# ScalarE's order inside a unit: first eviction, relu for two units ahead, second eviction, in place of the relu and then both evictions

## What is computed

```python
def _L0_gnn_ref(x, adj, W1, b1, W2, b2, gamma, beta):
    hi = einsum('bsh,hk->bsk', x, W1[:H])
    hj = einsum('bsh,hk->bsk', x, W1[H:])
    h = relu(hi[:, :, None, :] + hj[:, None, :, :] + b1)
    y = einsum('bijk,kl->bijl', h, W2) + b2
    y = _layernorm(y, gamma, beta)
    return einsum('bij,bijh->bih', adj, y)

x = _layernorm(x + L0(x, adj))
x = _layernorm(x + L1(x, adj))     # one attention head, weights exp(si + sj) * adj
```

## Time and profile before

| what | value |
|---|---|
| median of 3 executions | 2302.32 us (2300.99 to 2302.67) |
| the profiled execution, device time | 2303.22 us |
| its span, first to last instruction | 2301.4 us |
| mean granted TensorE clock | 0.998 |
| TensorE matmuls busy | 2280.2 us, 99% |
| TensorE weight loads busy | 2075.6 us, 90% |
| ScalarE busy | 2160.9 us, 94% |
| VectorE busy | 2145.2 us, 93% |
| GpSimd busy | 2016.9 us, 88% |

### The profile page before, as it was taken

The page is one execution under the profiler, slowest core; times in us unless marked ns, Lnnn a source line. Parts: engine busy times, 40 slices in busy tenths (PEclk is TensorE's granted clock), DMA queues, the critical chain, the costliest instruction groups (busy, mean ns, idle before and its releaser), DMA issues.

```text
span 2301.4 us, 168989 instructions
## 1 busy us (share of the span) xinstructions
PE 2280.2 (99%) x71248; PEld 2075.6 (90%) x71248; DVE 2145.2 (93%) x18262; ACT 2160.9 (94%) x3650; POOL 2016.9 (88%) x1227
## 2 busy tenths in 40 slices
PE   8999999999999999999999999999999999999997
PEld 8888888888888999999999999999999999999995
DVE  7999999999999999999999999999999999999998
ACT  8999999999999999999999999999999999999996
POOL 9898898888988988888888898898888988888884
PEclk9999999999999999999999999999999999999999
DMA  1000000000000000000000000000000000000000
GB/s 21 12 13 16 11 16 16 10 16 12 15 16 10 16 16 11 16 12 15 16 11 16 13 13 16 11 16 16 10 16 13 14 16 10 16 17 10 16 10 10
DMA packets 103862, 32.15 MB, mean 14 GB/s; under 512 B 77888, under 2 KB 103104, under 8 KB 103104
## 3 DMA queue, kind: packets, MB, share of 16 engines
q1 hardware_dynamic: 102240, 21.12, 4.4%
q10 hardware_dynamic: 864, 0.23, 0.0%
HBM read 17.11 MB, written 4.19 MB: 9 GB/s over the span
## 4 chain that ended last, share of the span: by engine, by line
PE 97%; ACT 2%; DVE 1%; POOL 0%; issue 0%; DMA 0%; SPq 0%; DVEq 0%; ACTq 0%
PE y_ps L567 76%; PE agg_ps L618 19%; PE work_ps L567 2%; ACT h L294 1%; ACT y L289 1%; POOL h L278 0%; DVE squares L553 0%; DMA b1c<-in_L_gnn_b_dram 0%; DVE o_sb L465 0%; DVE x_out L545 0%; POOL wz L269 0%; SPq L172 0%; DVE work_ps L483 0%; DVE work_ps L530 0%; DVE work_ps L479 0%
## 5 line engine op out<-in xcount | busy, mean ns | idle before, releaser
L278 POOL TENSOR_TENSOR h<-abT 128x1024 f32<-128x1024 f32 x1024 | 1944.0, 1919 | 239.3 <-PE y_ps L567 231.9
L567 PEld LDWEIGHTS y_ps<-w_pair,h 128*32 128x32 f32 x65536 | 1920.4, 110 | 173.6 <-issue 126.5
L567 PE MATMUL y_ps<-w_pair,h 128*32 128x128 f32 x65536 | 1966.0, 273 | 1.3 <-issue 0.6
L553 DVE CUSTOM_DVE_ANT_0 squares<-y_ps,y 128x128 bf16<-128x128 f32 x8192 | 1839.0, 284 | 110.4 <-ACT y L289 103.4
L289 ACT ACTIVATE y<-y_ps 128x508 f32<-128x508 f32 x2048 | 1137.5, 596 | 104.6 <-PE y_ps L567 97.6
L294 ACT ACTIVATE h<-h 128x1024 f32<-128x1024 f32 x1024 | 1089.3, 1064 | 2.4 <-POOL h L278 2.4
L553 DVE DVE_READ_ACCUMULATOR2_ANT q<- 128x1 f32 x8192 | 678.5, 83 | 0.0
L618 PE MATMUL agg_ps<-y,wz 128*32 128x512 f32 x4096 | 593.4, 592 | 3.2 <-DVE work_ps L483 3.1
L618 PEld LDWEIGHTS agg_ps<-y,wz 128*32 128x32 f32 x4096 | 180.4, 110 | 9.1 <-issue 9.1
L567 PEld LDWEIGHTS work_ps<-x1s,adjS 128*32 128x32 f32 x512 | 28.4, 110 | 31.5 <-issue 18.9
L252 POOL TENSOR_TENSOR wz<-adjT,rstd 128x128 f32<-128x128 f32 x64 | 34.8, 543 | 25.0 <-ACT rstd L325 25.0
(11 more groups left out here) (87 smaller groups left out, 591.3 us busy)
## 6 DMA issues: line engine op xcount, KB each, us to landing
adj_in<-in_adj_dram SPq DMA_DIRECT2D x256, 16.0 KB, 1.9
x_res<-in_x_dram SPq DMA_DIRECT2D x64, 64.0 KB, 2.1
adj_res<-in_adj_dram SPq DMA_DIRECT2D x64, 64.0 KB, 2.7
out_dram<-x_out SPq DMA_DIRECT2D x64, 64.0 KB, 1.9
x_in<-in_x_dram SPq DMA_DIRECT2D x254, 16.0 KB, 1.9
w1a<-in_L_gnn_W_dram SPq DMA_DIRECT2D x1, 64.0 KB, 1.9
w1b<-in_L_gnn_W_dram ACTq DMA_DIRECT2D x1, 64.0 KB, 2.2
w<-in_L_gnn_W_dram ACTq DMA_DIRECT2D x1, 64.0 KB, 2.3
```

Source lines behind the costliest of these rows:

```text
L278: nc.gpsimd.tensor_tensor(h[:, u % HRING].rearrange("k (r g) s -> k r g s", g=GROUPS), abT[:, p, 1, :].unsqueeze(1).unsqueeze(1).broadcast ...
L553: last = nc.vector.tensor_tensor_reduce(out=squares[:, (first_bank + k) % YRING, n, :], in0=y_ps[(first_bank + k) % YRING][:, n, :], in1=y ...
L567: last = nc.tensor.matmul(dst[cols], lhsT[:, cols], rhs, start=start, stop=stop, tile_position=(0, g * GROUP))
```

## The change

ScalarE's relu for unit u+2 moves from ahead of the unit's other work to between the unit's two evictions. No instruction is added or removed, no wait changes, and the other engines' programs stay as they are. The new order in a unit is: the unit's other work if it has any, E(2u), R(u+2), E(2u+1).

```diff
             def slot(t, half, p, pairs, prep, gather, tail, early, first_bank):
                 for u in range(UNITS):
-                    if pairs:
-                        ahead = u + 2
-                        if ahead < UNITS:
-                            relu(t, ahead)
-                        elif prep:
-                            relu(t + 1, ahead - UNITS)
                     if gather and u == 1:
...
                             act.wait_ge(y_in_psum, t * QUARTS + k + 1)
                             copy(y[:, p, k * QUART:(k + 1) * QUART, 0:LAST],
                                  y_ps[(first_bank + k) % YRING][:, :, 0:LAST]).then_inc(y_stored, 1)
+                            ahead = u + 2
+                            if k == u * QPU and ahead < UNITS:
+                                relu(t, ahead)
+                            elif k == u * QPU and prep:
+                                relu(t + 1, ahead - UNITS)
```

## The result

| | before | after |
|---|---|---|
| median of 4 executions each | 2302.29 us | 2336.1 us (2335.28 to 2336.51) |
| ratio after to before | | 1.0147, 95% interval 1.0136 to 1.0159 |
| span of the profiled execution | 2301.4 us | 2334.7 us |
| one slot in the middle | 35.47 us | 36.00 us |

The change costs 33.8 us. The forecast was 2345.9 us with a range of 2334 to 2356. The sign and the place were right; a slot loses 0.53 us, not 0.70.

The account below looks back on a forecast made before the run. The prediction took TensorE to bound the middle. A loss of 62 x 0.70 = 43.4 us plus 0.2 in the last slot, 43.6 us, on the median of 2302.32 gave 2345.9 us, range 2334 to 2356.

Parts of the forecast that it names:

- What bounds the kernel: Middle, 48.9 to about 2269 us: TensorE alone, 35.47 us a slot, so reordering ScalarE can only cost.
- R2 falls behind E0's wait, and R4 comes too late: Slot's start: ScalarE waits at E0 with R2 still to do; R4 lets unit 4 start 0.68 us late.
- The first rival: Relu late by one eviction only, hidden by 0.72 us of slack; time 2302 to 2303 us; chance 0.07.
- The steps from E0 to R4: ScalarE, units 0 to 2: relus 0.95, evictions 0.485, ln_v and rstd 0.60, beta_part 0.29 us; 1108.72 to 1114.99.
- The step after the wait: TensorE's start after a wait: 1.78 us to the next sum, not 1.746, adding 0.03 us a slot.
- When TensorE wants R4: Unit 4 due at 1114.36 in the slot starting at 1107.38; 0.72 us of slack for R4 before the change.
- R3's lateness: Unit 3: R3 lets TensorE go on 0.2 us late, contained in R4's 0.68.
- Slots times loss: Slots t = 2 to 63: 62 x 0.70 = 43.4 us.
- The last slot: Tail, units 11 to 13: VectorE gains 0.4 us, then waits and ends 0.2 us later; +0.2 us.
- E22: ScalarE's eviction, first of unit 11 in the last slot, at 2268.78; the count for units 11 to 13 goes from it.
- The rival of a second wait: R6 also late if single evictions or restarts cost more: 0.9 to 1.3 us a slot, 2358 to 2383 us; chance 0.06.
- R5, R6 and the banks: Other deadlines in the slot, claimed not late: slack 0.7 us for R5, 0.5 for R6, 1.4 for the bank.

Follow-up runs that it names:

- the run with unit 0 old: Kernel after the change, with the old order (R2, E0, E1) put back in unit 0 of each slot; 2304.54 us, ratio 1.0003 to the kernel before.
- The run with unit 2 new and one spare eviction: Kernel before, with the new order in unit 2 alone and one eviction that nobody reads ahead of E2; 2325.33 us, ratio 1.0096.
- the run with unit 1 old: Kernel after the change, with the old order (R3, ln_v, rstd, E2, E3) put back in unit 1 of each slot; 2335.2 us, ratio 1.0139 to the kernel before.

## Why the prediction was right, and where it was off

**What bounds the kernel**: right. TensorE fills the middle, and the reordering could only cost.

**R2 falls behind E0's wait, and R4 comes too late**: right, shown by the chain after and by the run with unit 0 old, which takes away this alone and gives all of the loss back. The first rival, a relu late by one eviction and hidden, would have been true without the wait for E0, but not by its own numbers. Without that wait R4 still moves behind `beta_part` and E4, and not by one eviction: in the run with unit 0 old it ends 6.87 us after the first matmul, and 154.20 - 148.15 = 6.05 before. These 0.82 us are more than the 0.72 of slack that the prediction had, and less than the 0.88 that R4 has.

**The steps from E0 to R4**: right to some hundredths. From E0's start to R4's end I had 1114.99 - 1108.72 = 6.27 us. After the change, E0 and R4 in the timeline of ScalarE:

```profile
1122.44 0.59 ACT L289 ACTIVATE y<-y_ps 128x508 f32<-128x508 f32 x1 [0.47 <-PE y_ps L566]
...
1127.63 1.06 ACT L294 ACTIVATE h<-h 128x1024 f32<-128x1024 f32 x1
```

And the same slot in the timeline of TensorE:

```profile
1121.25 7.24 PE L566 MATMUL y_ps<-w_pair,h 128*32 128x128 f32 x256
1128.75 1.95 PE L566 MATMUL y_ps<-w_pair,h 128*32 128x128 f32 x64 [0.25 <-ACT h L294]
1130.52 1.04 PE L617 MATMUL agg_ps<-y,wz 128*32 128x512 f32 x8
```

1128.69 - 1122.44 = 6.25 us. The evictions that stand singly cost 0.47 to 0.49 us, as in pairs. The Trainium skill's formula ("ScalarE: Activation LUTs", What ACT_TABLE_LOAD costs), from which the prediction estimated 0.516 us for an eviction, is not borne out here either. The step after the wait cost 1130.52 - 1128.75 = 1.77 against 1.746, 0.02 where I had 0.03. (The prediction's 0.68 and 0.03 add up to 0.71 and not to 0.70, which is 0.6 us in 62 slots.)

**When TensorE wants R4**: this is the term that was mis-sized. I took 1107.38 from the earlier trace rows as the first matmul's start and 1108.72 as E0's, 1.34 us apart. In the kernel after they are 1121.25 and 1122.44, 1.19 apart. An earlier slot of the kernel before began at 148.15, and the timeline of ScalarE there and in the last pair slot has E0 at:

```profile
149.34 0.59 ACT L289 ACTIVATE y<-y_ps 128x508 f32<-128x508 f32 x1
...
2245.05 0.59 ACT L289 ACTIVATE y<-y_ps 128x508 f32<-128x508 f32 x1
```

149.34 - 148.15 is 1.19 again. In the slot that I chose, 319 matmuls stand in one piece, the 320th stands among the sums, and the 8 sums fall into groups of 3 and 5. That is not the order of the program, so the rows of matmuls don't stand where they belong there, and TensorE's starts lie 0.15 us early against ScalarE's. No record is missing: the whole trace has 65536 of these matmuls, as many as the program. The expectations call a slot without such a mixture one with complete records. The length of a slot is not touched by this, but a distance between two engines is. With 0.15 us more, unit 4 is 0.52 us late and a slot loses about 0.54, and the trace has 0.53. The run with unit 2 new and one spare eviction bears it out: 0.37 us late, in a slot whose rows are in order. R3's lateness was too large by the same 0.15 us: the prediction had 0.2. In the run with unit 1 old, where R3 is on time, the first four units take 7.17 us and not 7.24, so R3 costs 0.07 us. As the prediction says, this is a part of unit 4's lateness and not a cost on top.

**Slots times loss**: from E0 to E0, the 59 slots from 149.34 to 2245.05 took 35.52 us each before and the 60 slots from 114.45 to 2274.71 (E0 of the last pair slot) took 36.00 each after. The 0.05 us over 35.47 are the 3 us of small stops that the earlier trace rows left over; in the kernel after they are nearly gone. Whether its waits took them in or there were none in this execution stays open. The prediction counted the loss from 35.47 and so did not have these 3 us. So the middle costs 62 x 0.484 = 30.0 us.

**The last slot**: VectorE's part was right. The chain of the kernel after, from E22 on:

```profile
2298.91 0.59 ACT y L289
...
2312.14 0.37 DVE work_ps L482
...
2312.64 7.32 PE agg_ps L617 x40
```

From E22's start to the end of `bias_added` it is 13.60 us; before it was 2282.10 - 2268.78 = 13.32. So 0.3 later, where I had 0.2. But then TensorE's last 40 sums took 7.32 us. Before, the rows of `bias_added` and of these sums read:

```profile
2281.73 0.37 DVE work_ps L483
2282.24 4.50 PE agg_ps L618 x40
```

Busy time of two stretches of the kernel before (PE, PEld, DVE, ACT, POOL), then TensorE's granted clock and two columns on DMA; the first stretch is TensorE's idle time, the second those sums:

```profile
2279.20:2282.20 3.00, 0.00 (x0) 0.00 (x0) 2.72 (x11) 1.08 (x3) 1.20 (x3) 1.00 0.00 0
2282.20:2287.00 4.80, 4.76 (x52) 1.98 (x56) 1.79 (x8) 1.10 (x4) 0.00 (x0) 1.00 0.00 0
```

The same two in the kernel after:

```profile
2309.40:2312.60 3.20, 0.00 (x0) 0.00 (x0) 2.89 (x12) 1.08 (x3) 1.20 (x3) 0.84 0.04 11
2312.60:2320.30 7.70, 7.66 (x52) 2.33 (x56) 1.84 (x9) 1.10 (x4) 0.00 (x0) 0.62 0.00 0
```

The granted clock was 1.00 there before and 0.62 after, which is 2.8 us. The sum is 30.0 + 0.3 + 2.8 = 33.1 us, against 33.3 between the two spans.

**That the number fell inside the range was partly luck.** The prediction says nothing of the clock in the tail. The measured 2336.1 us lie 2 us above the lower end of the range, 2334. The profiled execution had 2336.51, and without the 2.8 us of the clock it would have had 2333.7 (an estimate), just outside. The run with unit 1 old has the same slot of 36.00 us, and its profiled execution, with 4.50 us for the last 40 sums, took 2333.95. The mis-sized term is worth 62 x 0.15 = 9 us and the small stops 3 us, both too much in the forecast; the tail gave 2.8 us back.

**The rival of a second wait**: it did not come in the changed kernel, but a candidate was nearer than my text knew. I had checked R5, R6 and the banks, and not the sum's wait for `bias_added`. The change moves E4 ahead of R4 and so makes this deadline easier, from 0.25 us of slack to 0.85. E4 ends 6.5 us after the first matmul, not 6.8, and `bias_added` ends at 1129.52 in the slot shown above, whose sum starts at 1130.52 (1130.52 - 0.15 - 1129.52 = 0.85):

```profile
1129.16 0.36 DVE L482 SCALAR_TENSOR_TENSOR work_ps<-bias_rows,agg_ps,work_ps 128x128 f32<-128x128 f32 x1
```

That it stayed harmless was luck in the prediction.

## What to carry to other kernels

An instruction that stands ahead of a wait may be free, and behind the wait it costs in full: ask of a moved instruction what its engine did at that moment, not how many places it moves. List every deadline that the engine's outputs have in the tight stretch, those by way of a third engine too; here R4 (0.88 us of slack) hid E4, with 0.25. And take distances between two engines from a slot whose rows are in the program's order; the counts in the rows tell it.

## What the runs showed of the hardware

TensorE's clock in the tail is not the same in each execution. The last 40 sums follow an idle time of some 3 us, and took 4.50 us in six of the eleven profiled executions, 6.20 in two and 7.3 to 7.4 in three. The idle time before them, as the profile gives it, was 3.01, 3.08 and 3.36 us in executions with 4.50, and 2.94 and 3.31 us in ones with 6.20 and 7.43. The longer ones had a stretch at the lower of the clock's two levels, 1.2 in place of 2.4 GHz. In the three longest the granted clock fell during the idle time (0.80 to 0.85 over its last 3 us) and was 0.50 over the first 4.50 us of the sums; in the two of 6.20 us it was 1.00 during the idle time and 0.62 over those 4.50 us. The Trainium skill ("TensorE: Matmul & The Clock Gate", What's actually happening) says that idleness throttles the clock and that the phase of a free-running monitor decides when; that the same idle time gives both outcomes agrees with it, and no run here shows the monitor itself. It is worth up to 3 us, 0.1%, so differences of that size between two single executions of this kernel say nothing.
